# Gated delta rule on Trainium2: the moments' sums and the output projection leave the two-bank ring for P's banks, and half of the next q projection moves up beside k

## The reference, cut to what matters

```python
q = silu(causal_conv4(x @ Wq.T) + qcb); k = silu(causal_conv4(x @ Wk.T) + kcb) / 8
v = silu(causal_conv4(x @ Wv.T) + vcb)
a = sigmoid(x @ Wa.T + ba); beta = sigmoid(x @ Wb.T + bb)
for t in range(1024):                       # S: (batch, head, 64, 64)
    err = S @ k[t] - v[t]
    S = a[t][..., None] * S - beta[t] * outer(err, k[t])
    o[t] = S @ q[t]
o = layernorm_over_64(o) * ln_w + ln_b
x = x + (o * sigmoid(x @ Wg.T)) @ Wo.T
```

## Time and profile before

| | |
|---|---|
| median of 3 runs | 4022.02 us (4016.61 to 4035.32) |
| the profiled execution, its own time | 4030.5 us, its span 4028.7 us |
| recurrence | about 100 to 2430 us of the span, 64 chunks |
| busy over the span | PE 83%, DVE 80%, POOL 59%, ACT 51% |
| busy from 400 to 2450 us | PE 1693.6, DVE 1832.6, POOL 1528.4, ACT 843.5 of 2050 us |

### The profile page before, as it was taken

One profiled execution on the slowest core, in us unless ns is written; L12 is line 12 of the kernel. 1 busy time (PEld: TensorE's weight loads), 2 busy tenths in 40 slices (PEclk: granted clock), 3 DMA queues, 4 the chain that ended last, 5 costly groups with the idle time before them and its releaser, 6 DMA issues. The chain is left out here.

```text
span 4028.7 us, 110996 instructions
## 1 busy us (share of the span) xinstructions
PE 3360.8 (83%) x45505; PEld 2328.1 (58%) x45505; DVE 3228.1 (80%) x6024; ACT 2051.2 (51%) x4682; POOL 2376.9 (59%) x2981
## 2 busy tenths in 40 slices
PE   6888888888888888888888874668999989998998
PEld 4565655655656556556556553545666657655765
DVE  4999999889889988989898884227888878847885
ACT  4343444434434434444444432336888779827982
POOL 0777787777777767867777773432001078707860
PEclk9788888988888888889888885689999989998999
DMA  2111111111111111111111111410000011101110
GB/s 77 46 30 42 38 38 34 35 38 39 30 41 38 35 34 38 38 31 36 36 30 33 36 30 38 135 32 1 2 2 2 2 40 40 37 6 39 40 36 27
DMA packets 156104, 139.05 MB, mean 35 GB/s; under 512 B 65206, under 2 KB 108434, under 8 KB 155342
## 3 DMA queue, kind: packets, MB, share of 16 engines
q1 hardware_dynamic: 153294, 129.25, 11.7%
q0 software_dynamic: 2304, 2.71, 0.2%
HBM read 96.12 MB, written 16.82 MB: 28 GB/s over the span
## 5 line engine op out<-in xcount | busy, mean ns | idle before, releaser
L1123 DVE TENSOR_TENSOR a_tmp<-a_h,banks 128x128 f32<-128x128 f32 (+14 forms) x960 | 721.5, 752 | 33.6 <-POOL a_h L898 4.6
L1129 DVE TENSOR_REDUCE a_h<-a_tmp 128x64 f32<-128x128 f32 (+14 forms) x960 | 722.9, 753 | 26.4
L898 POOL TENSOR_TENSOR a_h<-a_h,a_a 128x128 f32<-128x128 f32 (+11 forms) x768 | 587.1, 764 | 136.8 <-DVE a_h L1129 127.0
L729 ACT ACTIVATE a_va<-banks 128x512 f32<-128x512 f32 x128 | 138.2, 1080 | 441.6 <-PE banks L544 441.6
L883 POOL TENSOR_TENSOR a_st<-a_st,a_ab 128x512 f32<-128x512 f32 x256 | 326.9, 1277 | 0.0
L530 PEld LDWEIGHTS banks<-a_xseg,a_w_k 128*128 128x128 f32 x2048 | 263.9, 213 | 51.8 <-DVE a_h L1129 26.0
L544 PE MATMUL banks<-a_w_v,a_xseg 128*32 128x512 f32 x2048 | 287.9, 713 | 0.0
L530 PE MATMUL banks<-a_xseg,a_w_k 128*128 128x128 f32 x2048 | 270.0, 297 | 9.0 <-DMA a_xseg<-xn 4.8
L1974 ACT ACTIVATE c_s<-c_s,c_low 128x384 f32<-128x384 f32 (+1 forms) x512 | 266.3, 579 | 18.9 <-DVE c_low L1918 13.5
L2019 POOL TENSOR_TENSOR c_qm<-c_qT,c_heads 128x512 f32<-128x512 f32 x32 | 33.3, 1040 | 396.1 <-PE banks L1843 395.8
L1918 DVE CUSTOM_DVE_ANT_0 c_s<-banks,c_band 128x384 f32<-128x384 f32 (+1 forms) x512 | 245.4, 517 | 23.6 <-PE banks L1843 23.6
(11 more groups left out here) (298 smaller groups left out, 8417.0 us busy)
## 6 DMA issues: line engine op xcount, KB each, us to landing
a_ab<-decays SPq DMA_DIRECT2D x512, 128.0 KB, 2.9
d_Vs<-d_V SPq DMA_DIRECT2D x128, 128.0 KB, 2.3
sent<-k_nothing SPq DMA_DIRECT2D x40, 64.5 KB, 2.4
b_xe<-sent SPq DMA_DIRECT2D x8, 322.5 KB, 3.5
a_xseg<-xn SPq DMA_DIRECT2D x32, 70.0 KB, 2.4
xn<-a_xnT SPq DMA_DIRECT2D x8, 256.0 KB, 2.8
a_xrow<-in_L_attn_x SPq DMA_DIRECT2D x128, 16.0 KB, 1.8
x<-a_xrow SPq DMA_DIRECT2D x128, 16.0 KB
```

The source lines that it names most:

```text
L898: e.tensor_tensor(self.history(ch, t + 1)[:, :, 0:t], self.history(ch, t)[:, :, 0:t], at, ALU.mult).then_inc(*self.s_hist.at((g, t)))
L1123: e.tensor_tensor(prod, both, gram, ALU.mult).then_inc(*step.at((g, t, "product")))
L1129: e.tensor_reduce(self.results(ch, t), prod, AX.X, ALU.add).then_inc(*step.at((g, t, "w")))
```

## The change

The mean's and the deviation's sums go to bank 4 and the output projection to bank 5, in place of the ring. They wait until DVE has transposed the chunk's P (`s_p2`), and the next P waits until they have been read. So the ring no longer waits for the moment that DVE reads after step 4, and holds three products less in a segment: `out`, `mean` and `dev` are no members of it. In the even chunk the mean comes after the time rows of k. The first half of the next q is projected (and brought back by ACT) in the even chunk behind k, in front of carry and U, and no longer in the odd chunk. k is held until step 9 and no longer until step 10.

```diff
--- before.py
+++ after.py
@@ -240,7 +240,7 @@
 assert R == 32 and SEG == 32
 PROJ = "qkvag"
 CONV = "qkv"
-HOLD = {"k": 10, "v": 9}
+HOLD = 9
 HAND = 4
 
 
@@ -510,8 +510,7 @@
         if len(self.ring) == n:
             self.ring.append(key)
         if n >= 2:
-            last = self.ring[n - 2]
-            q.wait_ge(self.s_moment if last[0] in ("mean", "dev") else self.s_evac, last)
+            q.wait_ge(self.s_evac, self.ring[n - 2])
         return self.c.bank(n % 2)
 
     def held(self, key):
@@ -578,10 +577,13 @@
 
     def pe_moment(self, e, q, s, which):
 
-        b = self.take(q, (which, s))
+        b, g = self.c.bank(4), 2 * s + 2 + (which == "dev")
+        if g < 2 * self.nseg:
+            q.wait_ge(self.s_p2, g)
         if which == "mean":
             q.wait_ge(self.s_o, 2 * s + 1)
         else:
+            q.wait_ge(self.s_moment, ("mean", s))
             q.wait_ge(self.s_squared, s)
         of = self.o2[s % 2] if which == "mean" else self.o1
         for m in range(8):
@@ -593,7 +595,11 @@
         self.pe_project(e, q, "g", s, half)
 
     def pe_out(self, e, q, s):
-        b = self.take(q, ("out", s))
+        b, g = self.c.bank(5), 2 * s + 5
+        if g < 2 * self.nseg:
+            q.wait_ge(self.s_p2, g)
+        elif s:
+            q.wait_ge(self.s_evac, ("out", s - 1))
         q.wait_ge(self.s_y, (s, 1))
         for ct in range(NCT):
             t = e.matmul(b[:, 0:D], self.y[:, ct, :], self.woT[:, ct, :],
@@ -607,6 +613,11 @@
             q.wait_ge(self.s_p2, g - 1)
         else:
             q.wait_ge(self.s_zeroed, 1)
+
+        if g >= 3:
+            q.wait_ge(self.s_moment, ("mean", s - 1) if ch else ("dev", s - 2))
+        if ch == 0 and s >= 3:
+            q.wait_ge(self.s_evac, ("out", s - 3))
         for pair in range(0, NB, 2):
             if g:
                 q.wait_ge(self.s_st if pair else self.s_state, (g - 1, pair + 1))
@@ -661,10 +672,10 @@
             old, older, nxt, g = s - 1, s - 2, s + 1, 2 * s
             more = nxt < self.nseg
             self.pe_P(e, q, s, 0)
+            for n in range(2):
+                self.pe_time_rows(e, q, s, n)
             if old >= 0:
                 self.pe_moment(e, q, old, "mean")
-            for n in range(2):
-                self.pe_time_rows(e, q, s, n)
             for n in range(2):
                 if older >= 0:
                     self.pe_turn(e, q, older, n)
@@ -674,9 +685,10 @@
             if more:
                 for half in range(2):
                     self.pe_project_rows(e, q, "a", nxt, half)
-                q.wait_ge(self.s_step, (g, HOLD["k"], "w"))
+                q.wait_ge(self.s_step, (g, HOLD, "w"))
                 for half in range(2):
                     self.pe_project(e, q, "k", nxt, half)
+                self.pe_project(e, q, "q", nxt, 0)
             self.pe_carry(e, q, g)
             self.pe_U(e, q, s, 0)
             g += 1
@@ -684,14 +696,13 @@
             if old >= 0:
                 self.pe_moment(e, q, old, "dev")
             if more:
-                for half in range(2):
-                    self.pe_project(e, q, "q", nxt, half)
+                self.pe_project(e, q, "q", nxt, 1)
                 for n in range(2):
                     self.pe_gram(e, q, nxt, n)
             if older >= 0:
                 self.pe_out(e, q, older)
             if more:
-                q.wait_ge(self.s_step, (g, HOLD["v"], "w"))
+                q.wait_ge(self.s_step, (g, HOLD, "w"))
                 for half in range(2):
                     self.pe_project_rows(e, q, "v", nxt, half)
             self.pe_carry(e, q, g)
@@ -776,7 +787,7 @@
         q.wait_ge(self.s_full, key)
         if s:
             q.wait_ge(self.s_add, s - 1)
-        e.activation(self.orow[:], self.held(key)[:, 0:D], ACT.Copy).then_inc(*self.s_evac.at(key))
+        e.activation(self.orow[:], self.c.bank(5)[:, 0:D], ACT.Copy).then_inc(*self.s_evac.at(key))
 
     def act_root(self, e, q, s):
         q.wait_ge(self.s_moment, ("dev", s))
@@ -843,11 +854,10 @@
             if more:
                 for half in range(2):
                     self.act_project(e, q, "k", nxt, half)
+                self.act_project(e, q, "q", nxt, 0)
             self.act_state(e, q, g)
             self.act_gram_bank(e, q, g + 1)
             self.act_gate_rows(e, q, g + 1)
-            if more:
-                self.act_project(e, q, "q", nxt, 0)
             if old >= 0:
                 self.act_root(e, q, old)
             if more:
@@ -1074,7 +1084,7 @@
             q.wait_ge(self.s_scaled, s - 1)
         if which == "dev" and s:
             q.wait_ge(self.s_root, s - 1)
-        e.tensor_reduce((self.mom if which == "mean" else self.var)[:], self.held((which, s))[:, 0:P].rearrange("p (i t) -> p t i", t=SEG),
+        e.tensor_reduce((self.mom if which == "mean" else self.var)[:], self.c.bank(4)[:, 0:P].rearrange("p (i t) -> p t i", t=SEG),
                         AX.X, ALU.add).then_inc(*self.s_moment.at((which, s)))
 
     def dve_reciprocal(self, e, q, s):
```

## The result

The changed kernel takes 3931.8 us (median of 4 runs, 3929.0 to 3937.2) where the kernel before, over four runs now, takes 4028.7: ratio 0.9759, 95% interval 0.9721 to 0.9798. The forecast was 3928. The profiled spans went from 4028.7 to 3932.7 us, by 96.0.

The account below looks back on a forecast made before the run. DVE's list was taken to bound the recurrence, plus PE late with U. 29 x (2.7 + 0.6) = 96 us off 4030.5 gives 3934.5, adjusted to the median 3926; forecast 3928, 8-in-10 range 3882 to 3982.

Parts of the forecast that it names:

- The bound: Recurrence: DVE's list sets the pace, plus PE late with U; the 119.0 us wait before L1161 falls to some 40.
- Odd chunk, 2.7 us: Odd chunk: half of q and the hole before `out` go, period 35.95 to 36.6 us for 39.0; gain taken as 2.7.
- the second branch of the same step: Odd chunk at the full clock: list ends near +25, PE idles 4 us, U and P run low; 0.6 us at worst.
- Even chunk, 0.6 us: Even chunk: turn begins 2.9 us earlier, half of q adds 3.74; early chunks gain, late stay; mean gain 0.6 us.
- The even chunk pays: Rival: q's 3.74 us lands on late even chunks, which lose 1.2 us; 44 us gained, 3978; chance 0.17.
- Nothing moves: Rival: late mean makes DVE's steps stand 2.4 us in each even chunk, eating the odd gain; 4015; chance 0.05.
- Both meet their best: Rival: clock stays up, DVE bounds both kinds of chunk; 4.6 of 5.1 us, 133 us, about 3889; chance 0.13.

Follow-up runs that it names:

- the filled hole: Kernel before, with 8 unread 128x128 matmuls put into the 2.4 us hole before the output projection, all waits kept: 3964.5 us, ratio 0.9852.
- the second profiled execution: The changed kernel run once more, nothing altered, against the kernel before: 3927.6 us, ratio 0.9766.
- output and mean moved: Kernel before with mean in bank 4, output in bank 5; dev in the ring, q whole in odd chunk, k held to step 9: 3935.2 us, ratio 0.9779.
- k from step 11: Mean and output in P's banks, q whole in odd chunk, k held to step 11 instead of 9: 3921.2 us, again 3918.8 us.

## Why the prediction was right

- *The bound.* Right: the gain came out of DVE's wait for U (119.0 to 28.6 us against the "some 40" foreseen), and P's wait did not change.
- *Odd chunk, 2.7 us.* Measured 2.9. Its places came true in part. Dev runs from +1.3 to +3.4, and root and table load stand before q's activations. q's half ends at +6.9 in 18 of the 27 chunks, later in the rest; the Gram is done at +11.5 on average (10.8 to 12.3) for +10.8, the output ends at +14.7 for +14.5. The term that was mis-sized is v: 13.1 us, the value of the one chunk that was read, where v averaged 12.0 over the odd chunks before and 10.2 after. So carry ended at +26.9 and not at +29.6, and the second branch of the same step, a PE that is early and U at the low clock, is what happened: PE was early in 24 chunks, and U took about 3 us or more in 16. Its price was put at 0.6 us at worst and is 0.3 (36.27 against 35.95), so the sum hardly moved. The Trainium skill's rule that I weighed there ("TensorE: Matmul & The Clock Gate", "A second HAM failure mode: psum-queue depth-cycling") agrees with the trace: the filled hole gave 60 us, and the clock rose from 0.50 to 0.92 in the stretch behind, as the last row of this text shows.
- *Even chunk, 0.6 us.* Measured 0.5 in the first and 0.6 in the second profiled execution, but not by the way that was forecast. The time rows' hole went, and turn and k came 3.9 and 4.0 us earlier on average. That is more than the 2.9 us read from one chunk, so that carry ended 0.6 us earlier and not 0 to 0.9 later. I had said that early chunks gain and late ones stay. In those late by more than 0.5 us DVE's wait fell from 26 us in all (10 of 25 chunks, 2.0 to 3.5 us late) to 18 (13 of 26, all but two of them 1.5 us late or less), in the second execution to 20; in the early ones with a slow U it fell from 7 to 4 and to 2 us. So at least half of the gain came where none was forecast.
- *The parts.* Alone they give 78, 23 and -45 us, 56 together; all three give 97. The half of q costs time by itself and is worth 40 us or more once mean and dev have left the ring. What it pays for then is dev's move: output and mean alone give 89. The forecast summed by chunk, not by part, and so had the total right, but it nowhere said that dev's move would cost and the output's would give most.
- *The rivals.* "The even chunk pays" did not come, but it is what the half of q does without the mean's move. "Nothing moves" needed a late mean: L1087 never waited. "Both meet their best" did not come either: 1.5 us of excess remain in the even chunk.

That the sum hit within 4 us is partly luck. In the odd chunk a v that was 2.9 us too long and a U that was too short nearly cancelled, since DVE's own work hides both; in the even chunk the late chunks gave what the early ones did not.

## What to carry to other kernels

A shared ring couples products that have nothing to do with each other: look for holes of PE that end with a reader of an unrelated tile, and move that product to a bank that is idle just then. Look at the wait that the new bank brings as well: for the output it was none, for dev it was P's transpose, and that move alone lost 1.5 us an odd chunk. Price a hole of PE twice, once as idle time and once as the low clock for the work behind it; filling the hole with useless matmuls measures the clock's part by itself. Finishing early is no aim in itself: in "output and mean moved" U took over 2.9 us for 1.99 in all 17 chunks in which PE had been idle for more than 4 us, and with k from step 11 in none of the 22 in which PE was at most 0.5 us early. Heavy work is best placed to end just as the other engine is ready; a hold that makes a hole for this won 14 us before k and lost some 30 before v.

## What was not expected of the hardware

The low clock came without a long idle time. In the chunk of the earlier trace rows PE idled 1.33 us, worked 1.88 us and idled again, and the granted clock fell about 0.3 us into this second hole of 2.43 us. PE then stayed at the lower level for 13.6 us, through the output and most of v's first half, though nothing interrupted them from 1028.9 us on:

```profile
1026.90:1040.40 13.50, 11.46 (x46) 5.37 (x50) 13.06 (x14) 5.28 (x10) 13.09 (x17) 0.50 0.17 54
```

In 25 of the 26 odd chunks with complete records the clock fell inside the second hole, between +13.3 and +15.0; how long it stayed low varied from 3.4 to 13.7 us. With 2.05 us of that hole filled it was 0.92 over the stretch that answers to the earlier trace rows:

```profile
1017.90:1024.00 6.10, 4.83 (x30) 2.66 (x34) 5.77 (x7) 3.37 (x7) 5.96 (x9) 0.92 0.03 5
```

Whether the kind of matmul in between counts too (the Gram's are small) is not shown.
